# Value products summed outside PSUM, a straight TensorE program and a new order of work in a two-layer attention kernel

## The reference

```python
# 1. attention of the first layer: one head of 128 channels, over the 1024 tokens
h = group_norm(x, norm_w, norm_b)                  # 8 groups
q, k, v = split(einsum('bchw,oc->bohw', h, qkv_w) + qkv_b)
x = x + proj(softmax(q @ k.T * 128**-0.5) @ v)
t = to_tokens(x)                                   # 1024 x 128
# 2. search and retrieval: 8 search heads, 2 retrievers, 16 channels a head
n = layer_norm(t)
attn = softmax(sq @ sk.T * 16**-0.5)               # 8 heads, 1024 x 1024
retrieved = einsum('bsij,brjd->bsird', attn, rv)   # 8 heads x 2 retrievers
gate = softmax(rq . (retrieved @ wk_ret) * 16**-0.5)   # over the 2 retrievers
t = t + (gate . retrieved) @ w_out
# 3. a linear layer with 4-bit codes (NF4), decoded with one scale for 16 codes
w_lora = NF4_TABLE[qidx] * scales
t = t + (layer_norm(t) @ w_lora.T) @ W.T
```

## Time and profile before

| | |
|---|---|
| median of 3 runs | 4802.08 us (4799.98 to 4807.84) |
| profiled execution | 4802.95 us |
| its span, first to last instruction | 4801.10 us |
| mean granted TensorE clock in it | 0.986 of full |
| busy: PE, PEld, DVE, ACT, POOL | 4608.7, 2533.9, 3906.7, 3317.4, 4242.2 us |
| DMA | 191.77 MB, 40 GB/s on the mean |

### The profile page before, as it was taken

One profiled execution on the slowest core, in us unless ns is written; L12 is line 12 of the kernel. 1 busy time (PEld: TensorE's weight loads), 2 busy tenths in 40 slices (PEclk: granted clock), 3 DMA queues, 4 the chain that ended last, 5 costly groups with the idle time before them and its releaser, 6 DMA issues.

```text
span 4801.1 us, 102107 instructions
## 1 busy us (share of the span) xinstructions
PE 4608.7 (96%) x29838; PEld 2533.9 (53%) x29838; DVE 3906.7 (81%) x8190; ACT 3317.4 (69%) x6657; POOL 4242.2 (88%) x1142
## 2 busy tenths in 40 slices
PE   5899999999999999999999999999999999999985
PEld 4555555555555555555555555555555555555532
DVE  4788888888888888888888888888888888888863
ACT  2567777777777777777767777767777777777654
POOL 1589999999999999999999999999999999999996
PEclk9899999999999999999999999999999999999987
DMA  1011111111111111111111111111111111111010
GB/s 33 23 45 45 50 32 45 32 45 45 49 32 45 32 45 45 49 32 45 32 45 45 49 32 45 32 45 46 49 32 46 31 45 49 45 32 49 24 40 14
DMA packets 92739, 191.77 MB, mean 40 GB/s; under 512 B 16744, under 2 KB 50920, under 8 KB 92400
## 3 DMA queue, kind: packets, MB, share of 16 engines
q1 hardware_dynamic: 92400, 186.45, 13.9%
HBM read 17.53 MB, written 16.78 MB: 7 GB/s over the span
## 4 chain that ended last, share of the span: by engine, by line
PE 85%; DVE 6%; ACT 4%; issue 3%; POOL 1%; SPq 0%; DVEq 0%; ACTq 0%; DMA 0%; POOLq 0%
PE ps_u L804 18%; PE ps_bank L769 13%; PE ps_bank L791 11%; PE ps_bank L755 10%; PE ps_bank L741 4%; PE ps_bank L679 4%; DVE max_part L1067 4%; PE ps_bank L690 3%; PE ps_bank L710 3%; ACT p L962 3%; PE ps_bank L813 3%; PE ps_bank L743 3%; PE ps_bank L744 2%; PE ps_bank L742 2%; DVE max_part L1051 2%
## 5 line engine op out<-in xcount | busy, mean ns | idle before, releaser
L645 POOL TENSOR_TENSOR p_sum<-p_sum,p 128x2048 f32<-128x2048 f32 x768 | 3510.8, 4571 | 363.6 <-ACT p L962 316.6
L1067 DVE TENSOR_REDUCE max_part<-ps_bank 128x1 f32<-128x512 f32 x4096 | 2570.5, 683 | 513.0 <-PE ps_bank L769 500.8
L962 ACT ACTIVATE p<-ps_bank 128x512 f32<-128x512 f32 x4096 | 2153.3, 612 | 564.4 <-PE ps_bank L791 553.4
L804 PE MATMUL ps_u<-p,rv 128*32 128x512 f32 x8192 | 996.8, 604 | 3.2 <-ACT u_sb L968 2.5
L769 PE MATMUL ps_bank<-k_stack,q_stack 63*128 63x512 f32 x4096 | 863.5, 451 | 65.4 <-DVE max_part L1067 17.7
L791 PE MATMUL ps_bank<-q_stack,k_stack 64*128 64x512 f32 x4096 | 839.8, 449 | 35.2 <-ACT p L962 20.2
L791 PEld LDWEIGHTS ps_bank<-q_stack,k_stack 64*128 64x128 f32 x4096 | 372.0, 186 | 518.9 <-ACT p L962 177.0
L645 POOL TENSOR_TENSOR p_sum<-p 128x2048 f32<-128x2048 f32 x128 | 584.1, 4563 | 69.3 <-ACT p L962 69.3
L769 PEld LDWEIGHTS ps_bank<-k_stack,q_stack 63*128 63x128 f32 x4096 | 372.4, 185 | 507.6 <-DVE max_part L1067 199.2
L755 PE MATMUL ps_bank<-v,p 128*128 128x129 f32 x4096 | 498.9, 277 | 2.6 <-ACT p L919 1.6
L755 PEld LDWEIGHTS ps_bank<-v,p 128*128 128x128 f32 x4096 | 471.9, 191 | 38.1 <-DVE t_front L1097 12.5
(11 more groups left out here) (139 smaller groups left out, 4475.8 us busy)
## 6 DMA issues: line engine op xcount, KB each, us to landing
k_stack<-k_hi SPq DMA_DIRECT2D x256, 128.0 KB, 2.6
q_stack<-q_hi SPq DMA_DIRECT2D x256, 128.0 KB, 2.8
x_sb<-in_x SPq DMA_DIRECT2D x32, 512.0 KB, 3.6
k_stack<-k_lo SPq DMA_DIRECT2D x128, 128.0 KB, 2.6
q_stack<-q_lo SPq DMA_DIRECT2D x128, 128.0 KB, 2.8
t_held<-t_front SPq DMA_DIRECT2D x32, 512.0 KB, 2.9
rqk<-tok_next SPq DMA_DIRECT2D x32, 512.0 KB, 3.6
t_core<-t_held SPq DMA_DIRECT2D x32, 512.0 KB, 3.9
```

The source lines that it names most:

```text
L645: pool.tensor_tensor(p_sum[:, phase % 2, :, :], before, p1[:, step % ring, :, :], ALU.add)\
L804: last = pe.matmul(ps_u[n * QUAD:(n + 1) * QUAD, :], rv[:, key_tile, :], p1[:, step % ring, n, :], start=(key_tile == 0), stop=(key_tile = ...
L962: act.activation(p1[:, step % ring, n, :], bank_of("scores", index // 2, n % 2), ACT.Exp, scale=scale1)\
L1067: dve.tensor_reduce(max_part1[:, phase % 2, i, n, half:half + 1], bank_of("max1", index // 2, side), AXIS.X, ALU.max)\
```

## The change

Six edits, made together.

- **Value products.** `ps_u` is gone, and `ps_bank` has eight banks. Every visit of `values` takes a bank of its own and accumulates only its two steps there. ScalarE copies the first visit of a phase to `u_sb` (`take_u`, in place of `evict_u`), and VectorE adds the three others to it (`add_u`, 12 an image). `u_sb` has two halves, one for each of two phases in turn.
- **Maxima.** `max_rows1` and `max_rows0` use one transpose each, of all the maxima at once, in place of four a phase and eight an image. The rows then lie on 16 (8) partitions of 128 elements: SP's `rows` copies take eight such pieces to two rows, and a new SP copy `row0` brings `max_row0` from `max_tile0` (ScalarE's copy of the transposed tile).
- **TensorE's program** is written out straight for all 35 turns (`loop=False`); the other engines keep their loops.
- **Order lists.** All five are new. In the TensorE list the turn is cut at another place, and more entries of one kind stand together.
- **Set-up.** The loads are shared between SP's and ScalarE's queues, `qkv_w` and the image first; TensorE transposes q's and k's weights as soon as they are there; decoding the NF4 codes moves behind `max0_last` of the first image, and the fold of the FFN weight into the bank of its last `value0`. The set-up tiles lie in `p1` instead of `p0`.
- **Small.** `prod` has one buffer; `mixed_channels` waits for phase 3 (first half) and 4 (second) in place of 2 and 4.

The core of the diff:

```diff
-BANKS = 7
+BANKS = 8
...
+value0.3@1/7 max_rows1.0@0/1 max1.16@0/43 max1.17@0/05 scores.62@-1/26 values.14@-1/1 scores.63@-1/74
+max1.18@0/23 max1.19@0/60 max1.20@0/51 scores.0@0/74 values.15@-1/2 scores.1@0/37 max1.21@0/64 scores.2@0/05
+scores.3@0/13 max1.22@0/67 max1.23@0/40 den.3@-1/5 turn_u.3@-1/2 max1.24@0/16 scores.4@0/37 scores.5@0/54
...
+value0.2@1 value0.3@1 max1.32@0 max1.33@0 max1.34@0 max1.35@0 add_u.14@-1 max1.36@0 max1.37@0 max1.38@0
+max1.39@0 max1.40@0 max1.41@0 max1.42@0 max1.43@0 add_u.15@-1 max1.44@0 max1.45@0 max1.46@0 max1.47@0 max1.48@0
...
+add.30@-1 add.31@-1 add.1@0 add.2@0 add.3@0 add.4@0 ln2_rstd.0@-1 add.5@0 add.6@0 add.7@0 add.9@0 add.10@0
+add.11@0 ln1_rstd.0@1 add.12@0 add.13@0 norm_rstd.0@2 add.14@0 add.15@0 add.17@0 add.18@0 add.19@0 add.20@0
+add.21@0 add.22@0 add.23@0 add.25@0 add.26@0 add.27@0 add.28@0 add.29@0
...
+take_rqk.0@0 store.0@-2 rows.1@0 rows.2@0 take.0@0 hold.0@1 stack.0@1 load.0@3 rows.3@0 row0.0@2 rows.0@1
+stack.1@1
...
+    if not loop:
+        for b in range(last + 1 - images, first + images):
+            turn_of(b)
+        return
...
-        setup_tiles = p0[:, :, :].rearrange("p a (b n) -> p (a b) n", n=P)
+        p1 = sb("p1", [P, ring, GROUP, HALF])
+        setup_tiles = p1[:, :, :, :].rearrange("p a g (b n) -> p (a g b) n", n=P)
...
-                sp.dma_start(q_index, qidx).then_inc(codes_loaded, 16)
-                sp.dma_start(block_scale[:, :], scales.rearrange("(o k) -> o k", o=P)).then_inc(codes_loaded, 16)
-                loads = [
-                    (qkv_rows, qkv_w.rearrange("(t o) c -> o t c", o=P)),
-                    (proj_rows, proj_w), (ffn_rows, ffn_w), (wq_r_sb, wq_r),
-                    (wq_sb[:, :], wq_s), (wk_sb[:, :], wk_s), (wv_r_sb[:, :], wv_r),
-                    (w_out_sb[:, :], w_out),
-                    (norm_cols[:, 0:1], norm_w.rearrange("(c a) -> c a", a=1)),
-                    (norm_cols[:, 1:2], norm_b.rearrange("(c a) -> c a", a=1)),
-                    (proj_bias, proj_b.partition_broadcast(P)),
-                ]
-                for to, source in loads:
-                    sp.dma_start(to, source).then_inc(weights_loaded, 16)
+                sp.dma_start(qkv_rows, qkv_w.rearrange("(t o) c -> o t c", o=P)).then_inc(qkv_loaded, 16)
+                sp.dma_start(x_sb[:, :], x_dram[0:1, :, :].rearrange("b c n -> (b c) n")).then_inc(x_loaded, 16)
...
+            @block.scalar
+            def _(act):
+                for to, source in ((proj_rows, proj_w), (wq_r_sb, wq_r), (wv_r_sb[:, :], wv_r), (ffn_rows, ffn_w),
+                                   (proj_bias, proj_b.partition_broadcast(P)), (wq_sb[:, :], wq_s),
+                                   (wk_sb[:, :], wk_s), (w_out_sb[:, :], w_out)):
+                    act.dma_start(to, source).then_inc(weights_loaded, 16)
+                act.dma_start(q_index, qidx).then_inc(codes_loaded, 16)
+                act.dma_start(block_scale[:, :], scales.rearrange("(o k) -> o k", o=P)).then_inc(codes_loaded, 16)
...
+                for n in range(2):
+                    last = pe.transpose(ps_bank[:, 1, n * P:(n + 1) * P], qkv_rows[:, n, :], ident[:, :])
+                last.then_inc(qk_turned, 1)
+                pe.wait_ge(weights_loaded, 16 * (11 + HEADS))
+                for n, source in enumerate((proj_rows, ffn_rows, wq_r_sb, wk_ret_blocks)):
+                    last = pe.transpose(ps_bank[:, 2, n * P:(n + 1) * P], source, ident[:, :])
                 last.then_inc(turned_filled, 1)
...
+                def row0(b, index):
+                    sp.wait_ge(max_tile0_ready, 1 * (b + 1))
+                    wait(sp, filled["score0"], halves * tiles * b)
+                    sp.dma_start(max_row0[0:1, :].bitcast(F32), max_tile0[:, :].bitcast(F32)).then_inc(row0_moved, 16)
...
+                        to = q_stack[ROWS - 1:2 * ROWS:ROWS, group * GROUP // 2 + pair, half * HALF:(half + 1) * HALF]
+                        heads = slice(2 * pair * tiles_per_half, 2 * (pair + 1) * tiles_per_half)
+                        sp.dma_start(to.bitcast(F32), max_row1[heads, :].bitcast(F32)).then_inc(rows_moved, 16)
...
-                    for i in range(tiles_per_half):
-                        last = pe.transpose(out[:, i * P:(i + 1) * P],
-                                            max_cols0[:, half * tiles_per_half + i:half * tiles_per_half + i + P], ident[:, :])
-                    last.then_inc(filled["max_rows0"], 1)
+                    out = open_bank(at[0], max_tile0_ready, 1, 1)
+                    pe.transpose(out[:, 0:P], max_cols0[:, 0:P], ident[:, :]).then_inc(filled["max_rows0"], 1)
...
-                        pe.wait_ge(max_row0_ready, halves * b + half + 1)
+                        pe.wait_ge(row0_moved, 16 * (b + 1))
...
+                    if b == 0 and query_tile == tiles - 1:
+                        pe.wait_ge(codes_decoded, 1)
+                        last = pe.matmul(out[:, 2 * P:3 * P], lora, turned[:, 1, :], start=True, stop=True)
...
-                    for i in range(tiles_per_half):
-                        last = pe.transpose(out[:, i * P:(i + 1) * P], max_cols1[:, GROUP * i:GROUP * i + P], ident[:, :])
-                    last.then_inc(filled["max_rows1"], 1)
+                    pe.transpose(out[:, 0:P], max_cols1[:, 0:P], ident[:, :]).then_inc(filled["max_rows1"], 1)
...
+                        pe.wait_ge(ffn_w_ready, 1)
                         pe.wait_ge(rv_ready, 1 * (b + 1))
-                    if 2 * visit % tiles == 0:
-                        wait(pe, u_evicted, phases * b + phase)
+                    part = visit % visits_per_phase
                     pe.wait_ge(p1_ready, weights_per_image * b + 2 * GROUP * (visit + 1))
+                    if part == 0:
+                        out = open_bank(at[0], u_taken, phases, phase + 1)
+                    else:
+                        out = open_bank(at[0], u_added, phases * u_adds, u_adds * phase + part)
                     for step in (2 * visit, 2 * visit + 1):
-                        key_tile = step % tiles
                         for n in range(GROUP):
-                            last = pe.matmul(ps_u[n * QUAD:(n + 1) * QUAD, :], rv[:, key_tile, :],
-                                             p1[:, step % ring, n, :], start=(key_tile == 0),
-                                             stop=(key_tile == tiles - 1))
+                            last = pe.matmul(out[n * QUAD:(n + 1) * QUAD, :], rv[:, step % tiles, :],
+                                             p1[:, step % ring, n, :], start=(step % 2 == 0), stop=(step % 2 == 1))
                     last.then_inc(values_done, 1)
...
-                }, banks)
+                }, banks, loop=False)
...
-                    act.wait_ge(filled["max_rows0"], halves * b + half + 1)
-                    act.copy(max_row0[0:QUAD, half * HALF:(half + 1) * HALF], bank_of("max_rows0", half)[0:QUAD, :])\
-                       .then_inc(max_row0_ready, 1)
+                def max_rows0(b, index):
+                    wait(act, row0_moved, 16 * b)
+                    act.wait_ge(filled["max_rows0"], 1 * (b + 1))
+                    act.copy(max_tile0[:, :], bank_of("max_rows0", 0)[0:tiles, 0:P]).then_inc(max_tile0_ready, 1)
...
-                def evict_u(b, phase):
-                    wait(act, filled["turn_u"], phases * b + phase)
-                    act.wait_ge(values_done, visits * b + (phase + 1) * visits // phases)
-                    act.copy(u_sb[:, :], ps_u[:, :]).then_inc(u_evicted, 1)
+                def take_u(b, phase):
+                    wait(act, filled["turn_u"], phases * b + phase - 1)
+                    act.wait_ge(values_done, visits * b + visits_per_phase * phase + 1)
+                    act.copy(u_sb[:, phase % 2, :], bank_of("values", visits_per_phase * phase)).then_inc(u_taken, 1)
...
+                    if b == 0:
+                        decode_ffn_weight()
...
+                    if b == 0 and i == tiles - 1:
+                        dve.tensor_copy(ffn_w_sb[:, :], bank[:, 2 * P:3 * P]).then_inc(ffn_w_ready, 1)
...
+                def add_u(b, visit):
+                    phase, part = divmod(visit, visits_per_phase)
+                    if part == 1:
+                        dve.wait_ge(u_taken, phases * b + phase + 1)
+                    else:
+                        dve.wait_ge(u_added, u_adds * (phases * b + phase) + part - 1)
+                    dve.wait_ge(values_done, visits * b + visit + 1)
+                    dve.tensor_tensor(u_sb[:, phase % 2, :], u_sb[:, phase % 2, :], bank_of("values", visit), ALU.add)\
+                       .then_inc(u_added, 1)
```

247 lines of the change are left out of this document (120 added, 127 removed).

## The result

The changed kernel takes 4849.49 us on the median (4842.70 to 4854.44), the kernel before 4801.8 in the same comparison: ratio 1.0096 (95% interval 1.0082 to 1.0109), 1% slower where 3.7% less was forecast. The profiled execution took 4854.44 us around a span of 4852.70.

The account below looks back on a forecast made before the run. TensorE, then GpSimd, bound the kernel; GpSimd's 134.7 us became a turn's floor. TensorE's 132.3 plus 6.2 of waits made 138.5 a turn; 29 turns (4016.5), 607 outside and 1.9 of surroundings gave about 4626 us, range 4560 to 4700.

Parts of the forecast that it names:

- Work of TensorE: TensorE's own work in a full turn: 137.5 us less 2.1 for 19 transposes and 3.1 for 16 tiling stays, 132.3.
- The sum's 0.68 us and GpSimd's 4.57: Each new VectorE sum was to take 0.69 us, and GpSimd's additions to stay at 4.57 us.
- The row by DMA: max_row0 through SBUF and an SP DMA: 0 to 1 us of wait before score0 a full turn, 0.3 taken.
- Set-up: Before the main program: shared load queues and later decoding bring the first statistics to 13.5 us, a gain of 8.8 us.
- Outside the full turns: Set-up, pipeline fill and drain together: 607 us instead of 628.
- 6.2 us of waits on TensorE: TensorE's waits in a full turn: the old 6.4, less 0.5 bubble and 1 bank and ps_u, plus 1 and 0.3.
- Fewer stays, 3.1 us saved: TensorE's stays in one tiling fall from 105 to 89 a turn, each about 0.2 us: 3.1 us saved.
- What waits for the new sums: TensorE waiting for banks that VectorE's twelve sums free: 0 to 8.3 us a turn, 1 us taken.
- The straight program: Unlooped TensorE code saves a 0.3 to 0.6 us bubble a turn; late code costs zero, with +0.5 as bound.
- "On SP only rows.0 stands behind it.": In SP's queue, only the rows.0 copy was said to stand behind the new max_row0 DMA; no time booked.
- GpSimd as the floor: GpSimd's unchanged 134.7 us of work a full turn, above TensorE's 132.3, was taken as the least a turn could last.
- The rival "slower": VectorE's twelve sums exposed, TensorE waiting 0.69 us at each, 8.3 a turn: turn 146.8, 4874 us; chance 0.09.

Follow-up runs that it names:

- rows_first: The changed kernel with SP's load of the next image moved behind rows.3 and row0: 4815.9 us, ratio 1.0025 to the kernel before.
- looped: The changed kernel with TensorE's program looped again instead of written out straight: 4826.4 us, ratio 1.0041 to the kernel before.
- rows_looped: The changed kernel with rows.3 and row0 ahead of SP's image load and TensorE's program looped: 4810.5 us, ratio 1.0013 to the kernel before.
- before_one_turn: The kernel before with one transpose a phase in place of four for the second attention's maxima: 4797.2 us, ratio 0.9983.
- rows_looped_fill: The changed kernel, rows ahead of SP's load, TensorE looped, plus six unread transposes behind those of max_rows1.3 and max_rows0: 4776.6 us, ratio 0.9944 to the kernel before.

## Why the prediction was wrong

**What held.** Work of TensorE: 608 matmuls and 16 stays fewer, and 3.3 of the 5.2 us a turn show once the consumers are fast. The sum's 0.68 us and GpSimd's 4.57. The row by DMA: in full turns score0 waits for it hardly at all (0.3 us was booked). Set-up: the first statistics start at 15.56 us, not 13.5, because the eight small loads of `wk_ret` land 3.0 us after their last issue (7.02 to 9.98), not 1.2:

```profile
3.35 3.67 SPq L405 DMA_DIRECT2D p<-in_L_attn_wk_ret  x8
...
9.98 1.12 PE L463 MATMUL ps_bank<-ident,p 128*128 128x128 f32 x4 [5.46 <-DMA p<-in_L_attn_wk_ret]
...
15.56 1.28 DVE L1033 BATCH_NORM_STATS2 stat<-x_sb 128x6 f32<-128x512 f32 x2 [0.32 <-PEq L393]
```

So 6.8 us gained, not 8.8. Outside the full turns the sum said 607, the trace 615.2.

**The step that failed** is the one that took 6.2 us of waits on TensorE over from the old turn. They are 13.8. The 7.4 us more than before lie, by the table, in three places: 5.0 more in the long runs (6.80 - 1.83), 1.6 less in the shorter ones, 4.0 more elsewhere. The long runs are the cause that the runs show best: 3.0 us came back at full clock when their consumers alone were halved, while the 5.0 are read from the trace. Of the 4.0 elsewhere the runs name, roughly, 0.5 for straight code (measured on the kernel before), 0.5 for SP's order and 1.3 for the clock (146.1 - 144.8). Some 1.7 us stay open.

- *Fewer stays, 3.1 us saved.* I read the gain of a longer run off and not its price, although held it: a run of two pairs that took 0.89 us for 0.66. A run of five or six pairs fills ten or twelve banks, of eight. This was in the order lists, in sight.
- *What waits for the new sums.* I looked at the sums' banks, 1 us; the pairs' banks were the ones that ran out. As a size for this list the 1 us was too much (0.2); for a list that isn't made for the sums it is far too little (4.3).
- *The straight program.* "I take zero, with +0.5": it was +0.5, the bound. The bubble of the earlier trace rows is gone, but a dozen other places lose more than it gave. Each wait for a bank now stands as 51 ns in TensorE's queue; that this is the reason isn't shown.
- *"On SP only rows.0 stands behind it."* True of row0, but the list also put `load.0@3` ahead of `rows.3@0`, quoted in the change, and I didn't ask what that load waits for. The Trainium skill (DMA: Bandwidth & Descriptors, section Queues, rings and completion order) says that on each of its engines descriptors are consumed in the order of their ring. The trace agrees: behind the load the rows landed 3.5 us after their issue, 0.4 us after the load itself, and in rows_first, ahead of it, after 2.2 us. How much of the wait is this and how much the later issue, no run separates.
- *The clock* stood nowhere in the sum, since it was full before. It was full with little to spare.
- *GpSimd as the floor.* Its 134.7 us were never reached: cut to half, the turn stayed. They were also 2.4 too high: the earlier trace rows has it busy 3703.20 / 28 = 132.3 us a turn, no more than TensorE's own work, and idle 11.6 us, not 9. The 4.64 us an addition came from a merged record; one takes 4.57.

The rival "slower" gave nearly the right number (4874, turn 146.8) for a wrong reason, by luck: exposed sums are 0.2 us a turn, not 8.3.

## What to carry over

An engine's saved work is time only if the order lets its consumers keep pace: when entries of one kind are put together, count the banks that a run fills against those that are free, at the consumers' pace, before booking the saved changes. Read every queue's list for what is moved past what, with what each moved entry waits for. And where a kernel runs at full clock, look at its thinnest stretch before taking matmuls out of it. When two versions are compared, lay their turns at full clock over each other first: a bubble at the loop's head or a spell can hide in the difference.

## What was not expected of the hardware

- Idle matmuls can keep the clock up: 0.65 us a turn of them ended all spells at half clock in full turns (10 of 29 before), worth 11 us. Taking three out of a thin stretch of the kernel before, with 0.3 us a turn less work, cost 21 us, of which 12 by spells and the rest by a longer wait for a DMA.
- The head of TensorE's loop holds a bubble of 0.4 to 0.9 us in some versions (`before`, looped, rows_looped) and none in others (before_one_turn, rows_looped_fill), with the same loop. It was 23 of the 34 us between the last two looped versions of the changed kernel.
- Written straight, both lists ran slower than looped: 14 us (before) and 23 us (changed, part of it by the clock), in steps of 0.05 to 0.10 us at a dozen places a turn. A wait for a bank is then an instruction of 51 ns, 180 to 195 times a turn; that this is the cause isn't shown.
- Relief is worth little in the wrong place: 86 shorter operations a turn gave 131 us, 170 others 63 (at full clock 3.0 and 1.3 us a turn).
